# Hybrid layer on one core: GpSimd adds the expert rows of two token blocks, and the work between the two FFN runs stands in another order

## The reference

```python
x = x + attn_a(layernorm(x))     # in-projection, causal conv, selective state space in chunks, gated norm, out-projection
x = x + ffn(layernorm(x))
x = x + layernorm(x) @ (weight * block_mask).T          # 512 x 512
x = x + ffn(layernorm(x))        # the same weights again

def ffn(h):
    g, u = split(h @ shared_w_gate_up.T)                # shared expert, 512 hidden values
    shared = (silu(g) * u) @ shared_w_down.T
    w, e = top_k(softmax(h @ gate_w.T), 2)              # 16 experts, 2 per token
    w = w / sum(w)
    return shared + sum_c w[c] * expert[e[c]](h)        # each 128 hidden values
```

## Time and profile before

| | |
|---|---|
| median of 3 runs | 2003.55 us (2002.83 to 2004.82) |
| profiled execution | 2019.41 us, of them span 2017.7 us |
| PE busy | 1966.0 us, 97% of the span |
| DVE busy | 1468.4 us, 73% |
| ACT busy | 1191.6 us, 59% |
| POOL busy | 1031.9 us, 51% |
| chain that ended last | PE 89%, DVE 6%, issue 2% |

### The profile page before, as it was taken

How to read it: one execution, slowest core, us unless ns; L and a number is a source line. 1 busy time by engine, 2 the same in 40 slices (tenths; PEclk the granted TensorE clock), 3 DMA queues, 4 the chain that set the end, 5 groups by cost and what they waited for, 6 DMA issues and landing times.

```text
span 2017.7 us, 38125 instructions
## 1 busy us (share of the span) xinstructions
PE 1966.0 (97%) x11776; PEld 1634.3 (81%) x11776; DVE 1468.4 (73%) x2764; ACT 1191.6 (59%) x2602; POOL 1031.9 (51%) x907
## 2 busy tenths in 40 slices
PE   5999999999999999999999999999999999989998
PEld 4888888888888888888888888888888878877886
DVE  7998499849975997599669866985798572177215
ACT  3786378538853884487449645964696435433441
POOL 1497059616951694179328922881398126240423
PEclk8999999999999999999999999999999999999999
DMA  2551135214512351234134312431353159932895
GB/s 92 165 169 57 44 120 171 61 37 125 161 52 64 112 156 43 87 109 136 43 92 129 112 43 93 148 102 33 98 161 93 33 178 354 333 95 74 325 371 159
DMA packets 143909, 253.92 MB, mean 126 GB/s; under 512 B 21448, under 2 KB 37832, under 8 KB 143696
## 3 DMA queue, kind: packets, MB, share of 16 engines
q1 hardware_dynamic: 134848, 231.35, 36.0%
q0 software_dynamic: 7520, 16.80, 2.7%
q10 hardware_dynamic: 1328, 3.15, 0.4%
HBM read 233.38 MB, written 25.69 MB: 128 GB/s over the span
## 4 chain that ended last, share of the span: by engine, by line
PE 89%; DVE 6%; issue 2%; ACT 1%; DMA 1%; another core or an unknown queue 1%; POOL 0%; DVEq 0%; ACTq 0%; SPq 0%; POOLq 0%
PE bank L1668 59%; PE bank L1787 7%; PE bank L1978 6%; PE bank L1801 5%; PE bank L1741 4%; PE bank L1990 3%; PE bank L1769 2%; DVE Y L1264 1%; PE bank L1965 1%; DVE spare L1361 1%; PE bank L1760 1%; PE bank L1808 1%; PE bank L1676 1%; DVE Y L1273 1%
## 5 line engine op out<-in xcount | busy, mean ns | idle before, releaser
L1668 PE MATMUL bank<-xh,wh 128*128 128x512 f32 x1288 | 523.9, 407 | 10.2 <-POOL wl L720 4.0
L1668 PE MATMUL bank<-xh,wl 128*128 128x512 f32 x1288 | 504.8, 392 | 0.0
L1668 PE MATMUL bank<-xl,wh 128*128 128x512 f32 x1288 | 503.0, 391 | 0.0
L720 POOL TENSOR_TENSOR wl<-raw,wh 128x512 fp32r<-128x512 f32 x144 | 192.6, 1342 | 462.6 <-ACT wh L877 462.6
L1264 DVE SCALAR_TENSOR_TENSOR Y<-bank,cpar,Y 128x511 f32<-128x511 f32 (+2 forms) x384 | 286.9, 747 | 23.5 <-ACT Y L921 14.3
L1668 PEld LDWEIGHTS bank<-xh,wh 128*128 128x128 f32 x1288 | 243.2, 189 | 60.5 <-POOL wl L720 4.9
L1668 PEld LDWEIGHTS bank<-xh,wl 128*128 128x128 f32 x1288 | 242.4, 188 | 54.1
L1668 PEld LDWEIGHTS bank<-xl,wh 128*128 128x128 f32 x1288 | 243.6, 189 | 45.7 <-issue 0.5
L737 POOL TENSOR_TENSOR Y<-Y,gt 128x512 f32<-128x512 f32 x128 | 183.6, 1434 | 94.5 <-DVE gt L1318 92.7
L1326 DVE TENSOR_TENSOR al<-Y,ah 128x512 fp32r<-128x512 f32 x128 | 95.9, 749 | 184.4 <-ACT ah L979 184.4
L1668 PE MATMUL bank<-wh,ah 128*128 128x512 f32 x544 | 213.6, 393 | 0.7
(11 more groups left out here) (231 smaller groups left out, 4033.8 us busy)
## 6 DMA issues: line engine op xcount, KB each, us to landing
mem<-c_rows SPq DMA_DIRECT2D x128, 256.0 KB, 3.8
mem<-wffn_d SPq DMA_DIRECT2D x62, 512.0 KB
E<-e_rows SPq DMA_DIRECT2D x256, 96.0 KB, 3.5
raw<-wconv_d SPq DMA_DIRECT2D x80, 256.0 KB, 2.9
cv<-c_rows SPq DMA_DIRECT2D x64, 256.0 KB, 4.0
spare<-c_rows SPq DMA_DIRECT2D x64, 256.0 KB, 4.1
raw<-wgate_d SPq DMA_DIRECT2D x64, 256.0 KB, 2.7
raw<-wout_d SPq DMA_DIRECT2D x64, 256.0 KB, 2.6
```

What stands on the lines that cost most here:

```text
L720: inc(pool.tensor_tensor(wl[:, W_SLOT[p], :], raw[:, R_SLOT[p], :], wh[:, W_SLOT[p], :], ALU.subtract), w_lo)
L1668: got = mm(out, l, r, start=first and n == 0, stop=last and n == 2)
```

## The change

Three things are edited.

The expert rows of token blocks 6 and 7 are added by GpSimd, in both runs, behind its last gather: for each block and each of the two experts it multiplies the gathered row block in place by its weight, waits for that, and adds it to `X`; a second semaphore `cmb_late` counts these additions. `BY_DVE = 6` blocks stay with VectorE. `combined` lets a reader wait for the semaphore that has its block.

VectorE: `combine(4)` goes ahead of the gate of the last hidden block, `combine(5)` behind the first means of the third norm; blocks 6 and 7 are gone. Between the runs, statistics of the fourth norm move ahead of low parts of the third.

ScalarE gets a written-out list `between_norms` in which the deviation of the third norm's second half stands ahead of weight pieces 4 and 5, and the fourth norm's first deviation ahead of the high part of block 7. TensorE transposes blocks 0 to 3 of the fourth norm ahead of the last projection.

```diff
--- before.py
+++ after.py
@@ -180,6 +180,13 @@
 
         ybuf = [quad[:, q // 2, q % 2 * HID:q % 2 * HID + HID] for q in range(Y_RING)]
 
+        def combined(eng, run, t):
+
+            if t < BY_DVE:
+                eng.wait_ge(cmb, 2 * BY_DVE * run + 2 * (t + 1))
+            else:
+                eng.wait_ge(cmb_late, 2 * (TT - BY_DVE) * run + 2 * (t - BY_DVE + 1))
+
         def back(c, t):
             return quad[:, t // 2, t % 2 * HID:(t % 2 + 1) * HID] if c else xn_row(t)
 
@@ -305,7 +312,9 @@
         mask_sum, mask_mm, mask_on = sem("mask_sum"), sem("mask_mm"), sem("mask_on")
         tx_mm, tx_ok = sem("tx_mm"), sem("tx_ok")
         tg_mm, tg_th, tg_hg, tg_h = sem("tg_mm"), sem("tg_th"), sem("tg_hg"), sem("tg_h")
-        ty_mm, ty_ok, cmb = sem("ty_mm"), sem("ty_ok"), sem("cmb")
+        ty_mm, ty_ok, cmb, cmb_late = sem("ty_mm"), sem("ty_ok"), sem("cmb"), sem("cmb_late")
+        scaled = sem("scaled")
+        BY_DVE = 6
         YB = (5, 6)
         DN_BANKS = ((4, 6, 7), (4, 5, 6, 7))
 
@@ -623,7 +632,7 @@
             ov = out_d.rearrange("(t p) h -> p t h", p=P)
             for t in range(0, TT, 2):
                 now(sp, dn_acc, 3, t + 2)
-                sp.wait_ge(cmb, 2 * TT + 2 * (t + 2))
+                combined(sp, 1, t + 1)
                 sp.dma_start(ov[:, t:t + 2, :], X[:, t:t + 2, :]).then_inc(out_done, 16)
             sp.wait_ge(out_done, 16 * (TT // 2))
 
@@ -795,6 +804,18 @@
                             back(c, t), None, slots_y,
                             bass.IndirectOffsetOnAxis(ap=slot[:, c * TT + t:c * TT + t + 1], axis=0),
                             bounds_check=TILES * P - 1).then_inc(ga_in[t], 16)
+                for t in range(BY_DVE, TT):
+                    pool.wait_ge(ga_in[t], 32 * (run + 1))
+                    now(pool, dn_acc, first, t + 1)
+                    n = 2 * (TT - BY_DVE) * run + 2 * (t - BY_DVE)
+                    for c in range(2):
+                        rows = back(c, t)
+                        pool.tensor_tensor(rows, rows, topw[:, t, c:c + 1].to_broadcast([P, HID]), ALU.mult
+                                           ).then_inc(scaled, 1)
+                        pool.wait_ge(scaled, n + c + 1)
+                        if c:
+                            pool.wait_ge(cmb_late, n + 1)
+                        pool.tensor_tensor(X[:, t, :], X[:, t, :], rows, ALU.add).then_inc(cmb_late, 1)
 
         @block.scalar
         def _(act):
@@ -1044,6 +1065,34 @@
             w_part(0, 4)
             w_part(0, 5)
 
+            def between_norms():
+                deviations(2, 0)
+                rows_norm(2, 1)
+                rows_norm(2, 3)
+                for t in range(CH):
+                    rows_high(2, t)
+                for p in range(NRAW):
+                    w_part(2, p)
+                deviations(2, 1)
+                rows_norm(2, CH + 1)
+                rows_norm(2, CH + 3)
+                rows_high(2, 4)
+                rows_high(2, 5)
+                w_part(2, 4)
+                w_part(2, 5)
+                rows_high(2, 6)
+                deviations(3, 0)
+                rows_norm(3, 1)
+                rows_norm(3, 3)
+                rows_high(2, 7)
+                for t in range(CH):
+                    rows_high(3, t)
+                deviations(3, 1)
+                rows_norm(3, CH + 1)
+                rows_norm(3, CH + 3)
+                for t in range(CH, TT):
+                    rows_high(3, t)
+
             def hidden_tanh(i, j):
                 now(act, g_mm, i, j + 1)
                 if j >= 2:
@@ -1079,8 +1128,7 @@
 
             for run in range(2):
                 if run == 1:
-                    layer_norm(2)
-                    layer_norm(3)
+                    between_norms()
                 first, second = 2 * run, 2 * run + 1
                 hidden_tanh(first, 0)
                 act.wait_ge(rt_dve, run * 3 + 2)
@@ -1138,7 +1186,7 @@
                         dve.wait_ge(x_in[t // 2], 16)
                     elif n == 2:
                         now(dve, dn_acc, 1, t + 1)
-                        dve.wait_ge(cmb, 2 * (t + 1))
+                        combined(dve, 0, t)
                     elif n == 3:
 
                         dve.wait_ge(pe_step, 6 + t)
@@ -1407,27 +1455,23 @@
                     inverse2(1)
                     xn2(4)
                     stats3(0)
-                    xn2(5)
                     lo2(4)
                     stats3(1)
                     xn2(6)
+                    stats3(2)
                     lo2(5)
-                    stats3(2)
-                    xn2(7)
-                    lo2(6)
                     stats3(3)
                     means3(0)
-                    lo2(7)
-                    stats3(4)
+                    lo2(6)
                     inverse3(0)
                     xn3(0)
                     xn3(2)
+                    lo2(7)
+                    stats3(4)
                     stats3(5)
-                    lo3(0)
+                    for t in range(CH):
+                        lo3(t)
                     stats3(6)
-                    lo3(1)
-                    lo3(2)
-                    lo3(3)
                     stats3(7)
                     means3(1)
                     inverse3(1)
@@ -1497,7 +1541,7 @@
                 def combine(t):
                     dve.wait_ge(ga_in[t], 32 * (run + 1))
                     now(dve, dn_acc, first, t + 1)
-                    n = 2 * TT * run + 2 * t
+                    n = 2 * BY_DVE * run + 2 * t
                     for c in range(2):
                         if c:
                             dve.wait_ge(cmb, n + 1)
@@ -1608,7 +1652,7 @@
                            None, ALU.is_gt).then_inc(mask_on, 1)
 
                 def combined_down(t):
-                    dve.wait_ge(cmb, 2 * TT * run + 2 * (t + 1))
+                    combined(dve, run, t)
                     add_down(second, t)
 
                 hidden(second, 0)
@@ -1620,8 +1664,8 @@
                 hidden_up(second, 2)
                 combine(3)
                 hidden_lo(second, 2)
+                combine(4)
                 hidden_gate(second, 3)
-                combine(4)
                 hidden_up(second, 3)
                 if run == 0:
                     stats2, means2, inverse2, xn2, lo2 = norm_parts(2)
@@ -1631,20 +1675,14 @@
                     combined_down(t)
                     if run == 0:
                         stats2(t - 1)
-                    if t == 1:
-                        combine(5)
                 if run == 0:
                     stats2(CH - 1)
                     means2(0)
-                combine(6)
+                combine(5)
                 if run == 0:
                     inverse2(0)
                     xn2(0)
-                    xn2(1)
-                combine(7)
-                if run == 0:
                     xn2(2)
-                    xn2(3)
                     lo2(0)
                     lo2(1)
                 for t in range(CH, TT):
@@ -1867,11 +1905,10 @@
                     for t in range(CH, TT):
                         project(t - 2)
                         transpose_rows(2, t)
-                    for t in range(6, TT):
-                        project(t)
-                        transpose_rows(3, t - 6)
-                    for t in range(2, CH):
+                    project(6)
+                    for t in range(CH):
                         transpose_rows(3, t)
+                    project(7)
                 pe.wait_ge(rt_ok, 2)
 
                 def router(b):
```

## The result

The changed kernel takes 2010.04 us (median of 11 runs, 2006.96 to 2013.29), the kernel before, run beside it, 2004.63 us (11 runs, 2002.49 to 2006.70). The ratio is 1.0027, with a 95% interval of 1.0020 to 1.0035: slower by 5.4 us, where 1.7 us faster was forecast. The time lies above the forecast range of 1995.5 to 2007.5 us.

The account below looks back on a forecast made before the run. The prediction took TensorE, holding 89% of the chain of waits, as the bound. It summed -3.3 us between the runs and +1.6 at the end to -1.7, from 2003.55 to 2001.8 us, range 1995.5 to 2007.5.

Parts of the forecast that it names:

- The end: Last 15 us, GpSimd's eight operations with no norm to hide them: +1.6 us, between -1.6 and +3.9.
- The slow rival: At the end, GpSimd's dependent chain takes 15.1 us and sets the finish: +4.8 us in all, 2008.4 us; chance 0.12.
- Step 1: Fifth pair ahead of the last gate: TensorE's matmul moves by at most -1.35 us, 0 if tanh isn't late.
- Step 2: GpSimd's eight operations behind its last gather in the first run: 10.6 us, hidden as far as readiness goes.
- Step 3: GpSimd holds VectorE operations with two SBUF inputs: +0.6 us on the hidden block, about +2.0 on the other three.
- Step 4: Hidden block to first projection: one pair less on VectorE -1.45, transposes' wait -0.8, exposed copies and low parts +0.6 us.
- steps 1 to 4: Everything up to the first projection after the third norm: -0.4 us, between -3.0 and +1.8.
- Steps 5 to 7: Third norm's second deviation, fourth norm's first rows, transposes ahead of the last projection: -0.4, -0.70 and -1.83 us.
- Step 5: Third norm's second deviation ahead of two weight pieces: TensorE's 0.71 us wait gets shorter, not gone, -0.4 us.
- The first stretch: From the first run's second shared FFN to the second run's router: -3.3 us, bounds -6.0 and -1.1.

Follow-up runs that it names:

- the second profile: The kernel before, unchanged, profiled again: 2003.11 us in a single run.
- experiment 4: The kernel before with two blocks' additions on GpSimd in the second run only, in the changed kernel's order there: 2012.87 us, ratio 1.0042.
- experiments 5, 6 and 11 to 15: Kernel before plus late GpSimd memset (1.0016, later 1.0036); four small copy kernels with 0, 8 or 94 gathers; changed kernel plus a GpSimd DRAIN per run (0.9978, 0.9998).
- experiment 8: Changed kernel with only the last block's additions on GpSimd in the first run and none in the second: ratio 0.9990.
- Experiments 2 and 16: The kernel before with only the work between the runs reordered, all additions on VectorE, measured twice: ratios 0.9979 (2000.05 us) and 0.9976.
- experiment 7: The kernel with only the work between the runs reordered, but the fourth norm's first transposes in their old places: 2002.57 us, ratio 0.9992.
- experiments 15 and 16: Changed kernel plus a GpSimd DRAIN ahead of each run's gathers (0.9978, then 0.9998); kernel before with only the work between the runs reordered (0.9976).
- experiment 9: Changed kernel with one block's additions on GpSimd in each run instead of two: ratio 1.0029.

## Why the prediction was wrong, point by point

**The end is the step that failed.** The forecast put +1.6 us there, between -1.6 and +3.9; it is +7.0. Two terms make it up. The last addition waits for GpSimd: it ends 3.8 us behind the last matmul instead of 0.8, so +3.0. That was foreseen, as the end of the range that holds if the tanh is on time (+3.9), and halved for no good reason: the profile's own span, 14 us above the timed runs, spoke against its lateness being theirs, and the second profile shows none. The other term, GpSimd's closing DRAIN, is in no step. In the changed kernel it adds 4.1 us (2002.4 to 2006.45), experiment 4 shows the same 4.1, and experiments 5, 6 and 11 to 15 show that it goes with GpSimd's last operation and with the gathers issued since the last DRAIN. It could have been read in the trace of the kernel before, 7.8 us behind the last gather.

**The slow rival** had the right place and nearly the right time (2008.4), but that is luck: its chain of 15.1 us is 10.2 us long (1988.43 to 1998.67) and gives +3.0 at the end instead of its +7.1. The DRAIN, which it doesn't have either, makes up the rest.

**Step 1** (0 if the tanh isn't late): it isn't, and TensorE doesn't wait for the last hidden block before (the second profile) or after. Worth 0.

**Step 2**, GpSimd's price: 10.3 us against 10.6, so nearly right. A multiplication by a repeated scalar takes 1.04, an addition 1.28 us.

**Step 3**, the holds: the mechanism was right, the size was not. For the sixth pair and the shift, +2.0 were forecast and 1.36 + 0.87 = 2.2 came. But the two normalizations were in no term. They have one large SBUF input, and were held for 1.75 us, 2.75 for two instead of the 1.00 of experiment 8. The Trainium skill has such a case (SBUF — State Buffer, section Who interferes with whom): a tensor_scalar can enter a two-port mode, and in that mode an instruction of VectorE contends with GpSimd too. The trace agrees in the lengths; it doesn't show the mode. The forecast used only the sentence on two SBUF inputs. The hidden block's low part, forecast at +0.6, wasn't held at all: with the tanh on time it starts at 1782.77, before GpSimd's first multiplication at 1784.41.

**Step 4**, one pair less and the eighth out of the way: TensorE's wait for the rows went from 0.98 to 2.40 us, so steps 1 to 4 come to +1.4 where -0.4 was forecast. The upper bound was +1.8. The sum closes: counted from VectorE's first addition of a down block, the means come 1.1 us sooner (5.9 instead of 7.0 us), the held pair and shift take 2.2 of it back, the held first normalization 0.8, and the second wait is 0.5 shorter.

**Steps 5 to 7**: the waits were 1.17, 0.72 and 1.83 us before, again, and all three are gone, -3.7 us against a forecast of -0.4, -0.70 and -1.83. Step 5 was sized too small: its wait went whole. Experiments 2 and 16 measured 4.2 and 4.8 us for the three together, experiment 7 the last of them.

The first stretch was thus forecast at -3.3 and is -2.3 us, inside its bounds. That is partly luck: too little gain in steps 1 to 4 and too much in step 5 offset each other.

**What stays open**: why the tanh is released late in some sets of runs and not in others. The profile names no releaser. The record numbers the chip of each set: the first, fourth and fifth set ran on the same number, with the kernel before at 2004.66, 2016.07 and 2004.43 us, so the chip alone doesn't decide it, as the expectations of experiments 15 and 16 supposed. Where it is late, the changed kernel with earlier DRAINs gains 0.22% instead of nothing, which fits a VectorE that has more to catch up on there, but no run separates that from other differences of those sets.

## What to carry to other kernels

Before work is given to an engine at the end of a program, look at what that engine does after its last operation: the closing line's instructions, by queue, show when each engine is really done, and what slack it has. Where GpSimd has issued many gathers, its closing DRAIN is long; let it be idle early, or drain it in an earlier pause that is long enough (here 21.6 us, of which the DRAINs took 6.8 to 7.6). And when a profiled execution is well above the timed runs, take a second profile before a term of the forecast is built on an oddity of the first.

## What the runs showed of the hardware

- GpSimd's closing DRAIN ends 0.08 us later for each gather issued since its last DRAIN, even when all of them landed 10 us before: 0.05, 0.72, 1.38 and 7.75 us behind GpSimd's last operation for 0, 8, 16 and 94. It runs from the end of that operation, be it a gather, an addition or a memset of 0.1 us (7.76 to 7.78 us in the large kernels with 94).
- The last gather of 128 rows lands 3.3 us after GpSimd is done issuing it at the end of experiment 9's kernel, and 2.5 us in its first run, so work on the last rows can't follow at once.
- GpSimd's and VectorE's operations hold each other: a 128x4 operation of 0.16 us took 1.03, normalizations with one large input (0.5 us) took 1.37 each, and GpSimd's 1.04 and 1.28 became 1.49 and 1.60. VectorE's statistics and its additions of a bank kept their 0.68 to 0.69 us.
- The same kernel took 2004 to 2005 us in three sets of runs and 2015 to 2016 in two, at a mean granted clock of 0.996 and of 0.994 to 0.995.
